# The load of a feed-forward group moved to the end of a step's DMA queue

## The reference, cut to what matters

```python
for i in range(DEPTH):        # 6 layers, 16 heads of 64, window 32
    x = attn_layer(shift_tokens(x), Wqkv[i], q_scale[i], k_scale[i], Wo[i]) + x
    x = ffn_layer(shift_tokens(x), ln_g[i], ln_b[i], W1[i], b1[i], W2[i], b2[i]) + x

def shift_tokens(t):          # the second half of the features comes from the token before
    a, s = jnp.split(t, 2, -1)
    s = jnp.pad(s, ((0, 0), (1, 0), (0, 0)))[:, :-1]
    return jnp.concatenate([a, s], -1)

def ffn_layer(x, g, bln, W1, b1, W2, b2):
    mu = x.mean(-1, keepdims=True)
    var = ((x - mu) ** 2).mean(-1, keepdims=True)
    xn = (x - mu) / jnp.sqrt(var + 1e-05) * g + bln
    hg = xn @ W1 + b1
    a, gate = jnp.split(hg, 2, -1)
    return a * jax.nn.gelu(gate, approximate=False) @ W2 + b2
```

## Time and profile before

| | |
|---|---|
| median of 3 runs | 2509.14 us (2507.46 to 2517.05) |
| profiled execution | 2509.24 us, its span 2507.4 us |
| TensorE busy | 2248.9 us, 90% of the span |
| VectorE, ScalarE, GpSimd busy | 70%, 71%, 56% |
| six-layer stack | about 330 to 1930 us of the span |
| DMAs | 141,473 packets, 96.74 MB, mean 39 GB/s |

### The profile page before, as it was taken

How to read it: one execution, slowest core, us unless ns; L and a number is a source line. 1 busy time by engine, 2 the same in 40 slices (tenths; PEclk the granted TensorE clock), 3 DMA queues, 4 the chain that set the end, 5 groups by cost and what they waited for, 6 DMA issues and landing times.

```text
span 2507.4 us, 87966 instructions
## 1 busy us (share of the span) xinstructions
PE 2248.9 (90%) x33272; PEld 1519.5 (61%) x33272; DVE 1744.5 (70%) x4841; ACT 1777.1 (71%) x6308; POOL 1400.8 (56%) x1358
## 2 busy tenths in 40 slices
PE   6998899999999999999999999999996756899996
PEld 4666466666666666666666666666663543566652
DVE  3554887778777777777787778777872236787853
ACT  3775687878777877877878877777873332788871
POOL 1664776666566666665666666666660002766640
PEclk9999899999999999999999999999997767999997
DMA  3000122112111122112211122112211000000000
GB/s 102 1 0 1 29 72 60 39 41 67 51 45 40 51 60 56 41 44 58 62 45 43 49 58 57 41 43 53 55 41 38 9 0 9 12 12 16 13 9 21
DMA packets 141473, 96.74 MB, mean 39 GB/s; under 512 B 61800, under 2 KB 133008, under 8 KB 141072
## 3 DMA queue, kind: packets, MB, share of 16 engines
q1 hardware_dynamic: 141072, 91.29, 14.4%
HBM read 23.11 MB, written 1.05 MB: 10 GB/s over the span
## 4 chain that ended last, share of the span: by engine, by line
PE 76%; ACT 8%; issue 7%; DVE 6%; POOL 2%; SPq 0%; DMA 0%; ACTq 0%; POOLq 0%; DVEq 0%
PE bank L715 21%; PE bank L826 8%; PE bank L736 7%; PE bank L793 6%; PE bank L770 4%; PE bank L880 4%; PE bank L862 3%; PE bank L871 3%; PE bank L779 3%; PE bank L389 2%; PE bank L700 2%; PE bank L764 2%; ACT arena L1313 1%; ACT L1313 1%; PE bank L838 1%
## 5 line engine op out<-in xcount | busy, mean ns | idle before, releaser
L715 PE MATMUL bank<-wqkv,hs 128*128 128x512 f32 x1344 | 673.9, 620 | 32.1 <-ACT arena L1291 15.3
L1491 POOL TENSOR_TENSOR arena<-arena 128x512 f32<-128x512 f32 x448 | 567.0, 1272 | 180.5 <-DVE arena L1630 180.1
L1498 POOL TENSOR_TENSOR arena<-arena,rnorm 128x512 f32<-128x512 f32 x448 | 454.4, 1042 | 381.8 <-DVE rnorm L1679 380.5
L1260 ACT ACTIVATE arena<-bank,amx 128x64 f32<-128x64 f32 x1536 | 457.6, 334 | 6.5 <-DVE amx L1694 6.1
L1625 DVE TENSOR_TENSOR arena<-bank,rot 128x512 f32<-128x512 f32 x448 | 307.0, 685 | 85.8 <-PE bank L715 83.1
L715 PEld LDWEIGHTS bank<-wqkv,hs 128*128 128x128 f32 x1344 | 229.7, 192 | 221.3 <-issue 159.8
L1237 ACT ACTIVATE arena<-bank 128x512 f32<-128x512 f32 x448 | 263.7, 616 | 126.4 <-PE bank L736 125.3
L1260 ACT ACTIVATION_READ_ACCUMULATOR arena<-bank,amx 128x1 f32 x1536 | 351.3, 229 | 0.0
L1630 DVE TENSOR_TENSOR arena<-bank,rot 128x256 f32<-128x256 f32 x896 | 333.8, 414 | 0.0
L1231 ACT ACTIVATE arena<-bank 128x512 f32<-128x512 f32 x448 | 265.2, 645 | 73.2 <-DVE arena L1630 72.1
L736 PEld LDWEIGHTS bank<-ident,arena 128*128 128x128 f32 x1792 | 213.1, 142 | 160.6 <-issue 127.7
(11 more groups left out here) (161 smaller groups left out, 3530.3 us busy)
## 6 DMA issues: line engine op xcount, KB each, us to landing
arena<-arena SPq DMA_DIRECT2D x768, 64.0 KB
wqkv<-in_L_ffn_Wqkv_dram SPq DMA_DIRECT2D x24, 256.0 KB
hs<-z SPq DMA_DIRECT2D x128, 32.0 KB, 1.8
fx<-z SPq DMA_DIRECT2D x32, 128.0 KB, 2.3
hs<-z SPq DMA_DIRECT2D x128, 31.8 KB, 1.9
fx<-z SPq DMA_DIRECT2D x32, 127.0 KB, 2.5
wqkv<-in_L_ffn_Wqkv_dram SPq DMA_DIRECT2D x24, 128.0 KB
w<-in_L_ffn_W_dram SPq DMA_DIRECT2D x6, 341.0 KB
```

Source lines behind the costliest of these rows:

```text
L715: nc.tensor.matmul(bank[o][:], src[:], wqkv[w][:, off:off + 512], start=True, stop=True).then_inc(AT[name] if part < 2 else AT[name][i], 1)
L1260: ins = nc.scalar.activation(pb[i][0][p % 2][:, h * DH:(h + 1) * DH], bank[3 + g][:, j * DH:(j + 1) * DH], ACT.Exp, bias=amx[p % 2][:, i, ...
L1491: nc.gpsimd.tensor_tensor(t, t, rs[i][c], ALU.add).then_inc(AT["ak" if c else "aq"][i], 1)
L1498: nc.gpsimd.tensor_tensor(t, t, rnorm[p % 2][:, i, HU * c:HU * c + HU].unsqueeze(2).to_broadcast([P, HU, DH]), ALU.mult).then_inc(AT["mk" ...
```

## The change

`shifted_group` is called last in a step and no longer between `shifted_batch` and `weights_part`. The load therefore stands behind the part of the weights and the four copies of unit 1. Nothing else moves, and no wait is added or taken away.

```diff
                     if s + 1 < hi:
                         shifted_batch(ph, s + 1)
-                    shifted_group(ph, s)
                     if ph["net"] == 0 and s % 16 >= 4 and s // 16 < 6:
                         weights_part(s // 16 + 1, s % 16 - 4)
                     if ph["net"] == 0 and lo <= s - 2 < hi:
                         turned_values(1, s - 2)
+                    shifted_group(ph, s)
```

## The result

The changed kernel takes 2524.12 us (median of 6 runs, 2518.61 to 2525.48) against 2508.30 (2502.32 to 2517.05) for the kernel before on the same chip. The ratio is 1.0056, with a 95% interval of 1.0036 to 1.0076: slower by 14 us. The forecast was 2521 us, the range 2509 to 2534. The loss is at the edge of what a measurement tells from no change, and its interval is clear of 1. The profiled execution took 2524.65 us.

A forecast was written before the change was run, and what follows sets the result against it. TensorE was taken to bound the kernel, with no transfer late. Shortfalls of 7.2 us plus 6 us for the instruction packet less 1.5 us given back made 11.7 us lost on 2509.24 us: 2521 us, range 2509 to 2534.

The forecast's parts named there:

- The bound and the mechanism: TensorE sets the end; the late load makes it wait at line 838 in 15 to 20 of 23 steps.
- Part 1: SyncE's queue: copies and weights go ahead of the load; nobody waits for them, so the gain is 0.
- Part 2: Load behind the copies, read at line 838: time needed against time there; shortfalls over 23 steps sum to 7.2 us.
- the need of 3.50 us: Last copy's end to line 838's matmul: 0.16 to issue, 0.50 between halves, 2.50 to landing, 0.34 to the matmul.
- Part 3: Instruction packet meets the load in ten steps; 0.33 us more each over 18 steps, 6 us, bounds 0 and 17.
- the small shortfalls: Ten steps with 3.35 to 3.46 us before line 838's matmul, short by 0.04 to 0.15, 0.7 in all.
- rival A: Packet and copies hold the load in most of 23 steps, about 1 us each: 26 us, 2535 us; chance 0.20.
- Part 4: Behind line 838, a stall gives back time of TensorE's later instruction halts: 1.5 us off, ends 0 and 3.
- The sum: Whole kernel: 7.2 + 6 - 1.5 = 11.7 us lost, 2521 us, bounds 2513 to 2533; chance 0.55.
- Rival B: Wait at line 838 hidden, or 3.50 us too high; large shortfalls count at half: 3 us, 2512 us; chance 0.20.
- C: Load and weights worsen TensorE's instruction stalls (lines 793, 764); new order gives -11 us, 2498 us; chance 0.05.

The follow-up runs named there:

- weights first: Against the kernel before, only the weights go ahead of the load, which stays ahead of the copies: ratio 0.9985, repeated 1.0000.
- the repeat: The changed kernel run once more, with no further edit, against the kernel before: ratio 1.0059 (1.0038 to 1.0080).
- The kernel with two copies ahead: As the changed kernel, but two of the four copies go behind the group load; ratio to the kernel before 0.9998 (0.9987 to 1.0009).

## Why the prediction was right, point by point

**The bound and the mechanism** hold. TensorE does no more work and waits at line 838 for the load in 18 steps (forecast: 15 to 20). The waits are longest in steps 6, 26, 46 and 74; steps 62 and 90, which the forecast had among the longest, lost 0.8 us each.

**Part 1, the weights and copies go first: 0 us.** The queue did as forecast (with weights in 17 of the steps and not 18), and nobody waits for these transfers. The price was off: "a transfer that nobody waits for gives nothing back" left out that its traffic can hold up the fetch of instructions. The halts ahead of line 838 fell by 3.5 us in the rows, by 2.6 in the repeat of weights first. The profile had the sign of it, "issue" as TensorE's largest wait, but not which traffic made it longer.

**Part 2, the need of 3.50 us.** The changed kernel shows 0.10 us to the issue, 0.59 between the halves, 2.50 to landing and 0.14 from landing to the matmul, 3.33 in all; the last term was taken too high, from a single place (0.34). In the 13 steps in which the copies are slow, or there is time to spare, the loss at line 838 is 7.0 us. The forecast had 6.5 for these (7.2 with the ten others).

**Part 3, what meets the load: 6 us.** In the other ten steps the load landed 3.56 to 4.78 us after the last copy, against 3.18 in most of the 13. The excess is 0.7 us each. Together with the small shortfalls these steps lost 6.3 us; 6.7 was forecast. The agreement is partly luck. The prediction said ten steps and then put 0.33 us on each of 18; the rows have 0.7 us in ten and next to nothing in the others. As a mean over all 23 loads that is 0.35, as the hs loads had, so the mean was a fair value, and rival A, a hold-up in every step, did not come true.

The delay is not where the forecast looked for it. Of the 7.4 us of excess, 6.2 are in SyncE's issue: one of the load's two issues took 1.0 to 1.5 us in each of the ten steps, in place of 0.54 or 0.63, and in nine of them the load then landed 1.9 to 2.0 us after the end of its second issue, as in steps without a packet; only step 26 landed clearly later (2.7). The rule of the Trainium skill (DMA: Bandwidth & Descriptors, Queues, rings and completion order), that an engine drains a whole packet before it turns to another queue, may be behind the long issues, but no run here shows it. What the rows show is that the excess goes with the instruction packet: in the first profile it is confined to the steps in which this packet passes as the last copy goes out, and in the repeat the load of step 70 too landed late (4.38 us after the last copy), with a second packet while it was under way.

**Part 4, 1.5 us given back** is the step that failed, by its sign: 1.7 to 3.5 us were lost there. I took it that a halt of TensorE lets the fetch catch up. (The test that the prediction had for this part, waits at 838 summing to more than the span grows, does not show it: 10.1 us against 15.4.) The matmuls of line 793 just behind the read in step 47, before (first) and after (second):

```profile
1039.70 0.32 PE L793 MATMUL bank<-arena 64*64 64x32 f32 x7 [0.69 <-issue]
```
```profile
1048.85 0.31 PE L793 MATMUL bank<-arena 64*64 64x32 f32 x7 [1.06 <-issue]
```

TensorE had just stood 0.95 us at line 838, and the halt got longer. Over the group steps these halts grew from 3.4 to 6.9 us, and to 5.1 in the repeat. All profiles with a load that is in time, or with three copies ahead of it, have 2.1 to 4.2, and all five with a late load 4.9 to 6.9. One reading is that the load and the copies are on their way when the next instruction packet is fetched; it was not tried by itself.

**The sum**: 7.0 + 6.3 at line 838, +1.7 to 3.5 of halts behind it, -3.5 ahead of it, together 11.5 to 13.3 us, where 11.7 was forecast and 14 (9 to 19) measured. Errors in parts 1 and 4 cancelled, so that the forecast came this near is in part luck; the wait at line 838 by itself was forecast at 13.2 and measured at 13.3.

The parts do not close to the microsecond. Between the residuals of steps 6 and 98 the profiled execution grew by 10.6 us and the repeat by 16.4; the granted clock of that stretch was 0.992 before, 0.996 in the first and 0.991 in the second, and the sum lies between the two. The span of the first grew by 15.4 us in all. Of the other 4.8 us 3.5 lie behind the stack, where no instruction was moved: 596.6 us against 593.1, at a granted clock of 0.846 against 0.854. The kernel with two copies ahead, which loses nothing at line 838, had 596.9 us there at 0.843, so this part belongs to the clock of the execution and not to the edit. Rival B (hidden) is out by the wait rows, though it was right that 0.34 us was too high; A is out by the ten steps. C had named the weights' traffic and the instruction halts, at 0.5 us for each step; the effect exists, at a third of that, and is smaller than the loss.

## What to carry to other kernels

A transfer has slack only up to a point: write down, step by step, the time from the end of what is put ahead of it to the moment of its read, and not the mean; here the fourth copy cost three times as much as the third, and the first two next to nothing. Put last in a queue what is read last: the copies had 6 us to spare and the load, read ahead of them, was sent behind them. A wait named "issue" on an engine with many small instructions is worth a look at what the DMA queues carry at that moment, even where nobody waits for these transfers.

## What was not expected of the hardware

Weight traffic whose issue ended 0.5 to 1.8 us ahead of a 16 KB packet of the instruction queue goes with a later start of that packet (0.3 to 1.4 us) and with halts of TensorE of 0.35 to 1.14 us in six of the steps, 3.0 to 4.4 us over the group steps, against 0.7 to 1.8 in all kernels without it, while four copies of 64 KB within SBUF in the same place do not add to them. The same packets lengthen an issue on SyncE that meets them, from 0.6 us to as much as 1.8 us. And a wait of TensorE did not shorten its next halt at "issue": after 0.95 us of standing, that halt was 1.06 us, 0.69 before. That these halts are for want of instructions is read from the packets beside them; the profile names no cause.
